# Layer-0 attention scores of a head pair, issued alternately on two halves of the TensorE array

## The reference, cut to what matters

```
# per batch: latents = norm(x), 256 x 256; context ctx, 256 x 192
q       = Wq latents                     # 4 heads of 64 channels
k, v    = from ctx (256 keys) and from the latents (256 keys): 512 keys
q, k    = rmsnorm over the 64 channels of a head
scores  = q k^T / 8                      # 4 heads x 256 queries x 512 keys
scores  = masked where mask is False     # the 256 context keys only
out     = softmax(scores) v
x       = x + tanh(g_xattn[0]) * (out Wo + bo)
```

## Time and profile before

| | us |
|---|---|
| median of 3 runs | 1278.59 |
| lowest, highest of them | 1276.69, 1280.53 |
| span of the profiled execution, first to last instruction | 1280.4 |
| layer-0 attention, cores of steps 1 to 14 (69.15 to 449.17 in the span) | 380.0 |
| mean granted TensorE clock over the span | 0.942 |

### The profile page before, as it was taken

The page is one execution under the profiler, slowest core; times in us unless marked ns, Lnnn a source line. Parts: engine busy times, 40 slices in busy tenths (PEclk is TensorE's granted clock), DMA queues, the critical chain, the costliest instruction groups (busy, mean ns, idle before and its releaser), DMA issues. The chain is left out here.

```text
span 1280.4 us, 30833 instructions
## 1 busy us (share of the span) xinstructions
PE 1146.8 (90%) x8451; PEld 900.4 (70%) x8452; DVE 793.8 (62%) x2494; ACT 598.8 (47%) x1400; POOL 425.2 (33%) x485
## 2 busy tenths in 40 slices
PE   3999999999999991899999999992999999369996
PEld 2688878888788871577777777772777777346674
DVE  5467888777888635244434444443688897647775
ACT  3455666556665530344444444441555555134442
POOL 2445665455655333000000000004466663202222
PEclk9799999999999965899999999995999999679999
DMA  4121211211111112222222222224684542334341
GB/s 129 52 84 46 68 60 63 86 58 67 61 62 54 49 41 75 62 75 79 81 78 78 78 82 78 79 65 145 216 241 150 168 156 77 112 95 105 109 109 58
DMA packets 94381, 116.20 MB, mean 91 GB/s; under 512 B 12479, under 2 KB 80049, under 8 KB 94066
## 3 DMA queue, kind: packets, MB, share of 16 engines
q1 hardware_dynamic: 82594, 84.50, 21.9%
q0 software_dynamic: 10576, 29.41, 6.7%
q10 hardware_dynamic: 1152, 1.58, 0.4%
HBM read 70.43 MB, written 45.92 MB: 91 GB/s over the span
## 5 line engine op out<-in xcount | busy, mean ns | idle before, releaser
L1380 DVE TENSOR_TENSOR e_z_low<-e_z_cols,e_z_high 128x256 f16<-128x256 f32 x142 | 60.0, 422 | 207.7 <-ACT e_z_high L1324 207.2
L1324 ACT ACTIVATE e_z_high<-e_z_cols 128x256 f16<-128x256 f32 x142 | 54.4, 383 | 250.3 <-PE e_z_cols L1296 250.3
L1047 PEld LDWEIGHTS a_out<-a_v_ones,a_probs 128*128 128x128 f32 x1024 | 125.7, 200 | 10.3 <-issue 10.1
L1047 PE MATMUL a_out<-a_v_ones,a_probs 128*128 128x65 f32 x1024 | 132.8, 285 | 0.0
L451 POOL DMA_INDIRECT z_rows<-r_z_tokens,r_slot_idx x96 | 98.6, 1027 | 70.2 <-ACT r_z_tokens L442 35.5
L1501 POOL IOTA a_first_numbers<- 128x2 int32 x1 | 0.1, 125 | 365.9 <-POOLq L68 365.9
L1390 DVE TENSOR_TENSOR e_hidden_low<-e_hidden_cols,e_hidden_high 128x384 f16<-128x384 f32 (+1 forms) x142 | 83.6, 589 | 36.4 <-ACT e_hidden_high L1339 36.4
L1286 PE MATMUL e_first<-w_high,e_z_high 128*128 x412 | 96.0, 314 | 4.3 <-DVE e_z_low L1380 3.5
L750 ACT ACTIVATE a_probs<-a_scores,a_latent_bias,a_k_scales 128x256 f32<-128x256 f32 x128 | 72.0, 563 | 54.3 <-POOL a_k_scales L683 41.7
L1286 PE MATMUL e_first<-w_high,e_z_low 128*128 x412 | 95.8, 314 | 0.0
L1286 PE MATMUL e_first<-w_low,e_z_high 128*128 x412 | 95.7, 314 | 0.0
(11 more groups left out here) (339 smaller groups left out, 3227.8 us busy)
## 6 DMA issues: line engine op xcount, KB each, us to landing
e_z_rows<-z_rows SPq DMA_DIRECT2D x142, 128.0 KB, 2.0
y_rows<-e_y_rows SPq DMA_DIRECT2D x103, 128.0 KB, 1.7
w_stage_first<-in_w SPq DMA_DIRECT2D x18, 352.0 KB, 3.0
a_ctx_in<-in_ctx SPq DMA_DIRECT2D x32, 192.0 KB, 3.6
e_token_rows<-z_rows SPq DMA_DIRECT2D x39, 129.0 KB
residual<-in_x SPq DMA_DIRECT2D x16, 256.0 KB, 3.4
z_rows<-r_z_tokens SPq DMA_DIRECT2D x16, 256.0 KB, 2.2
a_y_shared<-y_rows SPq DMA_DIRECT2D x16, 256.0 KB
```

The lines of the kernel that those rows point to most:

```text
L1047: ins = pe.matmul(O[t][:, h * (D + 1):(h + 1) * (D + 1)], pm[h % 2][:, jt, t * P:(t + 1) * P], va[p][:, jt, h, :], start=jt == 0, stop=jt ...
L1380: v.tensor_tensor(xl[p][:].rearrange("p k s -> p (k s)"), ZT[:, 0:KC * P], xh[p][:].rearrange("p k s -> p (k s)"), ALU.subtract).then_inc( ...
```

## The change

Heads are now taken in pairs: `score(m, p, pair, jp)` issues, for each key block and each pass, the matmul of the even head (partitions 0 to 63, bank `SC[0]`) and directly after it that of the odd head (partitions 64 to 127, bank `SC[1]`). A call makes 12 matmuls and fills both banks, so it waits until all exponentials of the call before are done. The number of matmuls, their sizes and the number of exponentials are the same as before. ScalarE's `head` becomes `pair_exps`: four exponentials per call, even and odd head in turn. TensorE's order changes as well: `products(0)` moves behind `project_qk`, next to `products(1)` and ahead of the second pair's scores, and `products(2)` moves behind `project_v_lat_key_sums` and `turn_q`, next to `products(3)`. Semaphore `scores` counts four groups per batch where it counted eight, and `products` waits for all eight exponentials of its pair.

```diff
@@ ScalarE @@
-                    act.wait_ge(scores, count(8 * (m - 1)))
+                    act.wait_ge(scores, count(4 * (m - 1)))
...
-                def head(m, p, h):
-                    for jp in range(2):
-                        if jp == 0:
-
-                            act.wait_ge(pv, count(4 * m + h - 1) if h else count(4 * m))
-                        act.wait_ge(scores, 8 * m + 2 * h + jp + 1)
-                        if h == 0 and jp == 0:
-                            act.wait_ge(s1_rr, m + 1)
-                        for j in range(2):
-                            jt = jp + 2 * (1 - j)
-                            b = maskf[:, ds(m, 1), jt] if jt < 2 else bias[:, 0:1]
-                            act.activation(pm[h % 2][:, jt, :], SC[jp][:, j * S:(j + 1) * S], ACT.Exp, bias=b,
+                def pair_exps(m, p, pair, jp):
+                    act.wait_ge(scores, 4 * m + 2 * pair + jp + 1)
+                    if pair == 0 and jp == 0:
+                        act.wait_ge(s1_rr, m + 1)
+                    for j in range(2):
+                        jt = jp + 2 * (1 - j)
+                        b = maskf[:, ds(m, 1), jt] if jt < 2 else bias[:, 0:1]
+                        for side in range(2):
+                            h = 2 * pair + side
+                            if jp == 0 and j == 0:
+                                act.wait_ge(pv, count(4 * m + h - 1) if pair else count(4 * m - 1 + side))
+                            act.activation(pm[side][:, jt, :], SC[side][:, j * S:(j + 1) * S], ACT.Exp, bias=b,
                                            scale=rr[p][:, jt * 4 + h:jt * 4 + h + 1]).then_inc(exps, 1)
...
-                        head(n, q, 0)
+                        pair_exps(n, q, 0, 0)
...
-                        head(n, q, 1)
+                        pair_exps(n, q, 0, 1)
...
-                        head(n, q, 2)
+                        pair_exps(n, q, 1, 0)
...
-                        head(n, q, 3)
+                        pair_exps(n, q, 1, 1)
@@ TensorE @@
-                def score(m, p, h):
-                    lo = (h % 2) * D
-                    for jp in range(2):
-                        i = 2 * h + jp
-                        pe.wait_ge(exps, count(16 * m + 2 * i - 2) if i else count(16 * m))
...
+                def score(m, p, pair, jp):
+
+                    i = 2 * pair + jp
+                    pe.wait_ge(exps, count(16 * m + 4 * i))
+                    if i == 0:
+                        pe.wait_ge(q_low, m + 1)
+                        pe.wait_ge(k_low, 2 * m + 2)
+                    for j in range(2):
+                        jt = jp + 2 * (1 - j)
+                        for x, w in PASSES:
+                            for side in range(2):
+                                lo = side * D
+                                ins = pe.matmul(SC[side][:, j * S:(j + 1) * S], kTs[p][w][lo:lo + D, pair, jt * P:(jt + 1) * P],
+                                                qTs[p][x][lo:lo + D, pair, :], start=x + w == 0, stop=x == 1)
+                    ins.then_inc(scores, 1)
...
-                    pe.wait_ge(exps, 16 * m + 4 * h + 4)
+                    pe.wait_ge(exps, 16 * m + 8 * (h // 2) + 8)
...
-                        score(n, q, 0)
+                        score(n, q, 0, 0)
...
-                        score(n, q, 1)
-                        products(n, q, 0)
+                        score(n, q, 0, 1)
...
-                        score(n, q, 2)
+                        products(n, q, 0)
                         products(n, q, 1)
+                        score(n, q, 1, 0)
...
-                        score(n, q, 3)
+                        score(n, q, 1, 1)
...
-                    if core:
-                        products(n, q, 2)
-                    if front:
                         project_v_lat_key_sums(f)
                         turn_q(f)
                     if core:
+                        products(n, q, 2)
                         products(n, q, 3)
```

## The result

The changed kernel takes 1361.3 us (median of 4 runs, 1359.3 to 1371.0) against 1278.3 before: 1.066 times as long, 95% interval 1.063 to 1.069. The profiled execution took 1359.3 us, its span is 1357.5. The direction was forecast, the size was not: 83 us more instead of 38, and outside the range, whose upper end was 1348.

The account below looks back on a forecast made before the run. TensorE's queue was taken to bound the kernel. Fourteen steps at 1.54 us of net waits plus 1.1 of clock falls gave 37 us, step 0 another 1.5: 1278.6 + 38.5 = 1317 us, range 1299 to 1348.

Parts of the forecast that it names:

- The bound, and what a score costs: Layer-0 attention: TensorE's queue sets the pace; twelve 64-row score matmuls take 1.41 us, 0.78 when paired.
- Rival C: Score calls: the halves run one after the other, 0.109 us a matmul; 1329 us, up to 1360 with falls; chance 0.20.
- Part 2, the lost double buffer: Steady attention step: calls wait for all four exponentials of the call before; 4.1 us of waits added, +1.54 net a step.
- the walk: Timing of one new attention step from its first score matmul: 4.52 us idle, ending at 28.68 against 27.14.
- Part 3, the clock: TensorE in the steady steps: clock falls in two steps of three, 1.7 us lost each, +1.1 us a step.
- The reasoning from `project_o`: After a fall, dense projections soon restore the clock, as behind `project_o` in the last step; hence 3 to 4 us at half.
- the far bound: Upper end of a fall's cost, from the last step before the change: 10 us at half clock, 5 us lost.
- The sum: Whole kernel: 14 steps x (1.54 + 1.1) = 37, plus 1.5 for step 0; 1278.6 + 38.5 = 1317 us.
- The small terms: Phase edges: 1.5 us more for step 0, 0 for step 15 (plus or minus 3).
- Rival A: Steady steps: scores overlap but the clock holds, 14 x 1.54 + 1.5 = 23 us more, 1302 us; chance 0.22.
- Rival D: ScalarE's exponentials overlap more when reading two banks in turn; not slower, 1278 to 1280 us or a little less; chance 0.08.
- The page's rule: TensorE's clock: small idle gaps between groups of matmuls can make it swing between levels; cited as speaking against the change.

Follow-up runs that it names:

- e2: Changed kernel with each call's six even-head matmuls first, then the six odd-head ones, no alternation: 1400.5 us, 1.094 of the kernel before.
- e1: Changed kernel plus 13 unread dense fp16 matmuls per step in the wait before scores (1,1): 1294.7 us, 1.013 of the kernel before.
- e8: Changed kernel plus 24 unread dense fp16 matmuls per step between `turn_q` and `products(2)`: 1369.8 us, 1.066 of the kernel before.
- e5: Changed kernel plus 13 unread dense fp16 matmuls per step behind scores (1,1), wait left open: 1312.3 us, 1.022 of the kernel before.
- e9: Changed kernel with `project_v_ctx` ahead of scores (1,1), `products(2)` ahead of `turn_q`, and ScalarE's `front_qk` before the weights' high-half copies: 1270.0 us, 0.992 of the kernel before.
- e10: Kernel before the change, with only ScalarE's `front_qk` moved ahead of the copies of the weights' high halves: 1274.8 us, 0.997 of the kernel before.
- e3: Changed kernel plus 13 unread fp32 matmuls of 65 columns per step in the wait before scores (1,1): 1316.8 us in one run.
- e11: e9 without alternation, the even head's six matmuls before the odd head's six in each call: 1283.2 us, 1.002 of the kernel before.

## Why the prediction was wrong

- **The bound, and what a score costs:** right. TensorE sets the pace, and the twelve scores of a call go from 1.41 to 0.76 (0.78 forecast). Rival C is out (e2, and the "x2" rows).
- **Part 2, the lost double buffer:** right. Each wait is where the walk put it, and the steps are 1.5 to 1.8 us longer with the clock up (e1 and the quiet steps) against 1.54 walked. The largest, before scores (1,1), is 1.64 from start to start against 1.69; the one before `turn_q` was walked too short, 0.11 for a bracket of 0.38. Costing ScalarE's order and the later `pv` at nothing held: no bracket names them.
- **Part 3, the clock:** the failing step. The prediction expected falls behind scores (1,1), and they are there, in 8 of 14 steps where I had taken two of three. But it took "3 to 4 us at half, 1.7 us lost" for each, on the ground that dense projections come soon. Measured: 20.5 us at half (17.1 once) and 6.9 to 7.3 us lost. The v projections, the first dense work behind the fall, did not lift the clock, nor did two calls of `products` in a row. The reasoning from `project_o` fails as well: in six of eight falls the clock was back before `project_o` of the next step began. So the ground for 3 to 4 us is gone, and what does end the stretch stays open; the runs show only that 24 dense fp16 matmuls put ahead of the products end it sooner (e8). The nearer row was the one I used as the far bound: about 10 us at half in the last step, with one call of `products`, `project_o` and some twenty scores before the rise.
- **The sum:** 14 x (1.54 + 1.1) should have been about 14 x (1.5 + 4.2), the 20.9 and 58.7 of e1, 79.6 together. The clock's term was short by 3.1 us a step, 43 us in all, which is nearly the whole miss of 44. The small terms came out otherwise too, but cancel: step 0 took 35.6 us against 30.0, 5.6 more and not 1.5, and began 2.0 us earlier; from step 15 to the end of the span 825.1 us passed against 831.2, 6.1 less and not 0. The span grew by 79.6 + 5.6 - 2.0 - 6.1 = 77.1.
- **Rival A** (clock holds, 1302) is what e1 shows with the gap filled: 1294.7. Rival D is out: in the quiet step the first four exponentials run from 368.47 to 370.28, still 0.45 each.
- **The page's rule:** The Trainium skill, TensorE: Matmul & The Clock Gate, section A second HAM failure mode: psum-queue depth-cycling, on micro-idle between groups and a swinging clock, agrees with the trace in what came of it, 8 falls in 14 steps with a gap of 1.44 us; but the gap alone does not do it, for e5 has the same gap and no fall. The Trainium skill, TensorEngine Tiling (Array Packing), section Key Properties, on tiles that run in parallel, agrees as well, with 0.109 us for two. The factor of up to 2 stands in that page's section Theoretical Speedup, and the trace has it in full, 0.109 us for two against 0.109 for one.

What stays open: which kinds of work bring the clock down or back, beyond the cases run here; and why of several steps with the same gap one falls and the next doesn't.

## What to carry to other kernels

Overlapping 64-row matmuls on both halves of the array really halves their time here, but two heads at once need both banks, and the double buffer that hid the exponentials is gone. Put work that is needed anyway (here the v projection) into the wait before you count the gain, and compare with the old order given the same tuning: e9 is only 0.05 us a step better than e10. On a TensorE that runs without gaps, price a new wait by what it does to the clock as well: with thin work beside it a gap of 1.4 us cost about that much waiting a step and 3.9 to 4.2 us of clock. And price a fall by the length of a measured low stretch, not by where the next dense work stands: that guess was some five times too short here.

## What had not been expected of the hardware

- At half clock TensorE was busy for all of 20 us and the clock did not rise, through fp16 projections with 64 and with 128 rows, key sums of 2 columns and 7 us of fp32 matmuls with 65 columns; it was back before the next dense projections in six of eight cases. 24 dense fp16 matmuls ahead of the products cut the stretch to 10.2 or 13.7 us (e8).
- The same fp32 form held a high clock in the same gap (e3), and so did dense work behind an open gap of 1.44 us (e5).
- A matmul for one half of the rows starts ahead of matmuls for the other half that were issued before it, by up to three (e11): 0.99 us for twelve that are not issued in turn.
